# Attention and expert scaling on one core: scaling image by image, set-up in another order, two of TensorE's waits one product earlier

## The chip, the cores and the metric

The kernel runs on one core of a Trainium2 chip. The metric is the device time of one execution in microseconds, the median of several runs. Three runs of the kernel before took 686.49, 684.30 and 683.94 us, so its time is 684.3 us.

## What is computed

The input is a batch of 8 images of 128 channels with 48 x 48 tokens. Two layers follow one another, each with a residual:

```python
# x: (8, 128, 48, 48); 8 heads of 16; feature(t) = elu(t) + 1
y = ln_over_channels(x)
Q, K, V = feature(y Wq + bq), feature(y Wk + bk), y Wv + bv      # the 8 heads of a token
den = 1 / (sum_d Q * cumsum(K, axis=1) + 1e-10)                  # here the sum runs over the heads
num = causal linear attention of Q, K, V over the 2304 tokens    # S += k v^T; o = q S
x = x + num * den
t = tokens of x
z = ln(t)
p = softmax(z @ gate_w + router_gamma)                           # 8 experts, the best two are kept
combine = the two largest of p, the rest 0
out = t + sum_e combine_e * (gamma_e * (z @ expert_w_e + expert_b_e) + beta_e)
```

The running sum of the keys in `den` runs over the 8 heads, not over the tokens: the reference sums along that axis, and the kernel adds 8 blocks of 16 columns.

## The kernel before

The work is cut into **groups**: one group is four images (U = 4) by 128 tokens, and 18 chunks of tokens by two halves of the batch make 36 groups. Each engine runs a hand-written list, called a step. Step k of an engine handles pieces of several groups at once: `at(age)` gives group k - age, so a piece written under `at(5)` belongs to the group that is five steps old. The order inside a step is the order of the lines in `step`, and it is the same in every step. Ten steps are written out ahead of a loop, 26 run in the loop, two in each turn, and six stand behind it. Waits between engines are semaphore waits that `need` writes, always on a count of groups. In the written-out steps (`g.edge`) some more waits are written, which the loop doesn't need.

A group goes through these pieces. On TensorE `x_transposed`, then four projections `project` (L1005 to L1007, three products each, with high and low parts of the numbers), `key_values` (L1081), `q_transposed` and `k_transposed`, `scores` (L1062), `from_state` (L1099), `values` (L1116), `x1_centred` (L1138, input of the router), eight `experts` rows (L1212 to L1214: four images by two halves of the experts, "a" for experts 1 to 4 and "b" for 5 to 8), `coef_transposed` (L1152) and `output` (L1226 to L1231). `key_values`, `from_state` and `values` work on small tiles of the array and begin with a load of unused weights (`blank`), behind their waits.

VectorE takes the token statistics (`statistics` L649, `variances` L657), reads the projections (`project` L667), makes the features (L674), the denominators (L680 to L691), masks the scores (`causal` L696), adds attention and residual (`attention` L715), runs the router's chain of small operations (L726 to L809), adds the four experts 1 to 4 of each image with their scales (`experts_1_to_4` L824, 16 instructions in a group) and writes the result (`residual` L834).

ScalarE scales experts 5 to 8 (`scaled_by_scalar` L497, 16 instructions in a group), copies between memories, and takes exponentials and squares. GpSimd subtracts for the low parts (`x_low` L298, L365), makes deviations (L305 and L307, L352 and L354), the running sum of keys (L314, L317, L323), the normalised queries (`qn` L329), the state (`middle` L339, `state` L345), the low part of the packed coefficients (`pack` L359), and adds the scaled experts of two images in one instruction (`add_parts` L373). SP issues all loads and stores.

The names of the trace: `wide_a` and `wide_b` are the four PSUM banks that projections, scores and experts share, so that the next projection of a bank waits until VectorE has taken the experts out of it. `bank_g` and `bank_o` hold the transposes, the router's input and the output. In the set-up VectorE makes masks, clears five buffers (L590 to L594) and prepares the projection's weights (`w_t` L599, `w_high`, `w_low`), and all of the first group's work stands behind that. The second set of weights is prepared in the first steps: `expert_weights` (L639, L642) on VectorE behind the first `attention`.

## Time and profile before

| | |
|---|---|
| median of three runs | 684.3 us |
| the profiled execution | 687.47 us, its span 685.7 us |
| TensorE busy | 623.9 us (91% of the span) |
| VectorE busy | 626.5 us (91%) |
| ScalarE busy | 437.5 us (64%) |
| GpSimd busy | 501.6 us (73%) |
| SP's transfers | 15.5% of the 16 DMA engines' span |

The time of an execution is a little above its span, which runs from the first instruction to the last. Busy time is a share over all stages: the kernel has a fill of some 65 us until the first group is scaled, a long even stretch, and a drain in which fewer and fewer pieces of work are left. In the even stretch the granted clock of TensorE is 1.00. A row of an order of time gives start, length, engine and line. A length is that of the instruction and not of its share of the engine: instructions overlap in the engine's pipeline, so what one costs is read from the distance to the next start.

### The profile page before, as it was taken

The page shows a single profiled execution, that of the slowest core. Times are in us where ns is not written, and L with a number is a line of the kernel's source. Part 1 is how long each engine was busy: PE and PEld are TensorE (multiplying, and loading weights), DVE is VectorE, ACT ScalarE, POOL GpSimd, SP SyncE. Part 2 cuts the span into 40 slices and gives each one's busy share as a digit, 9 for nine tenths or more (in the row PEclk, how much of TensorE's full clock was granted, in tenths as well). Part 3 has the DMA queues.
Part 4 walks back from the last instruction along what each step waited for, and adds up shares of the span by engine and source line. Part 5 has one row for each costly group of instructions (what it writes and reads, how often), then busy time and mean ns, then how long its engine had stood idle before and what let it go on. Part 6 is the DMA issues. An engine that isn't in the chain of part 4 may idle for free.

```text
span 685.7 us, 37586 instructions
## 1 busy us (share of the span) xinstructions
PE 623.9 (91%) x13936; PEld 506.3 (74%) x14044; DVE 626.5 (91%) x2175; ACT 437.5 (64%) x1549; POOL 501.6 (73%) x745
## 2 busy tenths in 40 slices
PE   4769989999999999999999999999999999998875
PEld 3657777777777777777777777777777777777663
DVE  6778989999999999999999999999999999999774
ACT  1337656666667777666666667776776666667643
POOL 4747767777778888887778877878787787766631
PEclk9989999999999999999999999999999999999997
DMA  5211110111111111111111111111111121111001
GB/s 131 78 34 34 34 48 8 47 49 50 47 46 46 46 46 46 46 46 46 46 46 46 46 46 46 46 46 46 46 46 46 46 62 31 32 34 34 19 19 31
DMA packets 60234, 30.58 MB, mean 45 GB/s; under 512 B 2160, under 2 KB 60176, under 8 KB 60176
## 3 DMA queue, kind: packets, MB, share of 16 engines
q1 hardware_dynamic: 60176, 29.79, 15.5%
q8 instruction: 39, 0.64, 0.4%
q14 instruction: 19, 0.16, 0.1%
HBM read 20.34 MB, written 9.44 MB: 43 GB/s over the span
## 4 chain that ended last, share of the span: by engine, by line
PE 52%; DVE 24%; issue 15%; POOL 5%; DVEq 1%; ACT 1%; POOLq 0%; ACTq 0%
DVE total L824 4%; PE wide_b L1005 4%; PE num L1116 4%; PE wide_a L1212 4%; PE num L1081 3%; PE num L1099 3%; PE wide_a L1213 3%; PE wide_a L1214 3%; DVE bn L649 3%; DVE probs L696 3%; PE wide_a L1062 3%; DVE o L834 2%; PE bank_g L1037 2%; PE bank_g L975 2%; PE bank_g L1022 2%
## 5 line engine op out<-in xcount | busy, mean ns | idle before, releaser
L497 ACT ACTIVATE part<-wide_a,scale 128x128 f32<-128x128 f32 x576 | 156.3, 382 | 2.5 <-PE wide_a L1214 1.0
L373 POOL TENSOR_TENSOR two_sums<-part 128x512 f32<-128x512 f32 x72 | 92.9, 1290 | 32.0 <-ACT part L497 30.4
L1212 PE MATMUL wide_a<-e_high,x_high 128*128 128x512 f32 x216 | 97.8, 453 | 3.1 <-issue 1.1
L460 ACT ACTIVATE q_eo<-bank_g,parity 128x512 f32<-128x512 f32 x72 | 49.7, 690 | 67.5 <-PE bank_g L1037 67.5
L1214 PE MATMUL wide_a<-e_high,x_low 128*128 128x512 f32 x216 | 85.6, 396 | 0.0
L1213 PE MATMUL wide_a<-e_low,x_high 128*128 128x512 f32 x216 | 85.4, 395 | 0.0
L317 POOL TENSOR_TENSOR k_sum<-k_sum,feat 128x64 f32<-128x64 f32 x216 | 72.6, 336 | 16.9
L359 POOL TENSOR_TENSOR pack<-weight,pack 128x64 fp32r<-128x64 f32 x36 | 22.2, 616 | 77.1 <-ACT pack L505 77.1
L824 DVE SCALAR_TENSOR_TENSOR total<-wide_b,scale,total 128x128 f32<-128x128 f32 x216 | 58.8, 342 | 0.0
L824 DVE SCALAR_TENSOR_TENSOR total<-wide_a,scale,total 128x128 f32<-128x128 f32 x216 | 58.8, 342 | 0.0
L1212 PEld LDWEIGHTS wide_a<-e_high,x_high 128*128 128x128 f32 x216 | 41.6, 193 | 21.1 <-issue 17.2
L1116 PE MATMUL num<-probs,v_pad 64*32 64x64 f32 x4608 | 54.1, 225 | 2.4 <-issue 1.2
L674 DVE SCALAR_TENSOR_TENSOR feat<-ex,qkv 128x512 f32<-128x512 f32 x72 | 51.7, 718 | 0.0
L298 POOL TENSOR_TENSOR x_low<-x,x_high 128x512 fp32r<-128x512 f32 x36 | 47.0, 1305 | 4.6 <-ACT x_high L421 4.6
L448 ACT ACTIVATE k_t<-bank_g 128x512 f32<-128x512 f32 x36 | 21.5, 597 | 44.7 <-PE bank_g L1022 44.7
L427 ACT ACTIVATE ex<-qkv 128x512 f32<-128x512 f32 x72 | 44.6, 622 | 8.4 <-DVE qkv L667 8.3
L1116 PEld LDWEIGHTS num<-probs,v_pad 64*32 64x32 f32 x4608 | 47.8, 105 | 1.8 <-issue 1.4
L1062 PE MATMUL wide_a<-q_eo,k_t 32*64 32x128 f32 x1152 | 41.9, 275 | 7.0 <-issue 3.7
L323 POOL TENSOR_TENSOR qk<-k_sum,feat 128x512 f32<-128x512 f32 x36 | 45.9, 1276 | 2.8
L1214 PEld LDWEIGHTS wide_a<-e_high,x_low 128*128 128x128 f32 x216 | 40.9, 189 | 9.6
L667 DVE SCALAR_TENSOR_TENSOR qkv<-wide_a,rstd,b_qkv 128x384 f32<-128x384 f32 x72 | 43.7, 609 | 4.5 <-issue 3.6
L365 POOL TENSOR_TENSOR x_low<-x,x_high 128x512 fp32r<-128x512 f32 x36 | 46.1, 1280 | 0.0
(175 smaller groups left out, 2003.6 us busy)
## 6 DMA issues: line engine op xcount, KB each, us to landing
x<-in_x SPq DMA_DIRECT2D x36, 256.0 KB, 3.0
x_res<-in_x SPq DMA_DIRECT2D x36, 256.0 KB, 3.6
out<-o SPq DMA_DIRECT2D x36, 256.0 KB, 3.1
e_raw<-in_L_ffn_expert_w SPq DMA_DIRECT2D x1, 512.0 KB
beta_raw<-in_L_ffn_beta_w SPq DMA_DIRECT2D x1, 512.0 KB
w_raw<-in_L_conv_Wkv SPq DMA_DIRECT2D x2, 64.0 KB, 2.4
b_qkv<-in_L_conv_bkv SPq DMA_DIRECT2D x1, 128.0 KB, 5.9
w_raw<-in_L_conv_Wq SPq DMA_DIRECT2D x1, 64.0 KB, 2.6
```

Of the source, the lines that this page charges most:

```text
L298: tt(x_low[:, g.par], x[:, g.par], x_high[:, g.par].bitcast(F32), ALU.subtract)\
L317: tt(k_sum[:, :, h], k_sum[:, :, h - 1], f[:, :, 1, h], ALU.add).then_inc(S["cumsum"], 1)
L373: tt(two_sums[:, g.par, two], part[:, two, 0:2], part[:, two, 2:4], ALU.add).then_inc(S[f"two_sums{p}"], 1)
L460: nc.scalar.activation(q_eo[:, g.par, :, e], bank_g[:].rearrange("p (u t) -> p u t", t=T), copy, scale=parity[:, e:e + 1]).then_inc(S[done ...
L497: last = nc.scalar.activation(part[:, u, e], w_bank[B_BANK[u]][:, 128 * e:128 * e + 128], copy, scale=scale[:, g.par, u, 4 + e:5 + e])
L674: stt(feat[:, g.par, 2 * h:2 * h + 2], ex[:, 2 * h:2 * h + 2], 1.0, qkv[:, g.par, 2 * h:2 * h + 2, 0:256], ALU.min, ALU.max).then_inc(S[f" ...
L824: last = stt(total[:, g.par, u], w_bank[A_BANK[u]][:, 128 * e:128 * e + 128], scale[:, g.par, u, e:e + 1], before, ALU.mult, ALU.add)
L1062: last = mm(w_bank[h][at, T * u:T * u + T], k_t[rows, g.par, u, at], q_eo[rows, g.par, u, :, at], start=True, stop=True, skip_group_check= ...
L1116: last = mm(num[PAIR * h:PAIR * h + PAIR, first:first + SUB], v_pad[at, g.par, u, 2 * h + e], probs[at, g.par, h, u, e], start=False, stop ...
L1212: mm(out, x1_high[:, g.par, u], e_high[:, four], start=True, stop=False)
L1213: mm(out, x1_high[:, g.par, u], e_low[:, four], start=False, stop=False)
L1214: mm(out, x1_low[:, g.par, u], e_high[:, four], start=False, stop=True).then_inc(S[f"{'ab'[half]}_{u}"], 1)
```

## The change

The edits are these.

- **Unit steps for the scaling.** `experts_1_to_4` takes one image instead of a pair. Experts 1 and 2 are added onto the first half of the sum of ScalarE's parts and experts 3 and 4 onto the second half, in two partial totals, and `output` transposes the two totals of an image instead of a total and a half. `add_parts` on GpSimd adds the parts of one image, 256 elements, instead of a pair. Semaphores `two_sums`, `a_steps` and `a_sum` exist for each image.
- **Set-up.** GpSimd clears the state, the padded values and the coefficients, which VectorE did before, and VectorE copies the transposed weights ahead of the small placement copies.
- **One instruction to another engine.** The addition of 1e-10 to the denominators is done by ScalarE instead of VectorE.
- **TensorE's waits.** For `key_values` and `values` the waits stand in front of the last product of the row ahead (a projection, an expert's row), and their load of unused weights is left out. In the written-out steps both stay. `from_state` follows `scores` at once and keeps both.
- **Order.** All five engines get another order of the pieces in a step, and ages that fit it. On VectorE the ages of most pieces fall by one, which only says where its step begins. SP stores a result in the step of its group's age 6 instead of 9 and loads the residual at age 2 instead of 4.

The diff, cut; the lists of the steps are told by the rows of order below it.

```diff
@@ -291,17 +291,21 @@
             made(nc.gpsimd.memset(blank[:], 0.0))
             for e in range(EXPERTS):
                 made(nc.gpsimd.memset(order[:, :, e:e + 1], float(EXPERTS - e)))
+            made(nc.gpsimd.memset(state[:], 0.0))
+            for b in range(PAR):
+                made(nc.gpsimd.memset(v_pad[:, b], 0.0))
+                made(nc.gpsimd.memset(coef_t[:, b].bitcast(F32), 0.0))
...
-            def add_parts(g, p):
-                need(pool, f"part{2 * p}", g.i + 1)
-                need(pool, f"part{2 * p + 1}", g.i + 1)
+            def add_parts(g, u):
+                need(pool, f"part{u}", g.i + 1)
                 need(pool, "out_done", g.i - 1)
-                two = slice(2 * p, 2 * p + 2)
-                tt(two_sums[:, g.par, two], part[:, two, 0:2], part[:, two, 2:4], ALU.add).then_inc(S[f"two_sums{p}"], 1)
+                tt(two_sums[:, g.par, u], part[:, u, 0:2], part[:, u, 2:4], ALU.add).then_inc(S[f"two_sums{u}"], 1)
...
+            def denominators_eps(g):
+                need(act, "rden_done", g.i)
+                need(act, "den_sum", g.i + 1)
+                nc.scalar.activation(den1[:], den[:], copy, bias=1e-10).then_inc(S["den_eps"], 1)
...
@@ -586,20 +596,15 @@
                 for g in range(PAIRS):
                     rows = slice(PAIR * g, PAIR * g + PAIR)
                     copy(mask32[rows], heads_mask[rows, rows]).then_inc(done, 1)
-                for b in range(PAR):
-                    nc.vector.memset(v_pad[:, b], 0.0).then_inc(done, 1)
-                nc.vector.memset(state[:], 0.0).then_inc(done, 1)
                 nc.vector.memset(ins_window[:], 0.0).then_inc(done, 1)
-                for b in range(PAR):
-                    nc.vector.memset(coef_t[:, b].bitcast(F32), 0.0).then_inc(done, 1)
+                dve.wait_ge(S["first_pe"], 1)
+                copy(w_t[:], w_bank[0][:, 0:384]).then_inc(done, 1)
                 for n in range(2):
                     copy(place[:, n].rearrange("e (k j) -> e k j", j=2 * EXPERTS)[:, :, EXPERTS * n:EXPERTS * n + EXPERTS],
                          ident[0:EXPERTS, 0:EXPERTS].unsqueeze(1).broadcast_to([EXPERTS, EXPERTS, EXPERTS])).then_inc(done, 1)
-                dve.wait_ge(S["first_pe"], 1)
-                copy(w_t[:], w_bank[0][:, 0:384]).then_inc(done, 1)
                 dve.wait_ge(S["first_pe"], 2)
                 copy(w_high[:], w_bank[1][:, 0:384]).then_inc(done, 1)
-                dve.wait_ge(done, 19)
+                dve.wait_ge(done, W_READY - 1)
                 tt(w_low[:], w_bank[1][:, 0:384], w_high[:].bitcast(F32), ALU.subtract).then_inc(done, 1)
...
-            def experts_1_to_4(g, p):
+            def experts_1_to_4(g, u):
                 need(dve, "out_done", g.i - 1)
-                need(dve, f"two_sums{p}", g.i + 1)
+                need(dve, f"two_sums{u}", g.i + 1)
                 need(dve, "scale_done", g.i + 1)
-                need(dve, f"a_{2 * p}", g.i + 1)
-                need(dve, f"a_{2 * p + 1}", g.i + 1)
-                done = S[f"a_steps{p}"]
-                for e in range(4):
-                    for k in range(2):
-                        u = 2 * p + k
-                        if e > 0:
-                            dve.wait_ge(done, 6 * g.i + 2 * e - 1 + k)
-                        before = total[:, g.par, u] if e > 0 else two_sums[:, g.par, u, 0]
-                        last = stt(total[:, g.par, u], w_bank[A_BANK[u]][:, 128 * e:128 * e + 128],
-                                   scale[:, g.par, u, e:e + 1], before, ALU.mult, ALU.add)
-                        if e < 3:
-                            last.then_inc(done, 1)
-                last.then_inc(S[f"a_sum{p}"], 1)
+                need(dve, f"a_{u}", g.i + 1)
+                done, y = S[f"a_steps{u}"], w_bank[A_BANK[u]]
+
+                def add(e, before):
+                    return stt(total[:, g.par, u, e // 2], y[:, 128 * e:128 * e + 128], scale[:, g.par, u, e:e + 1], before,
+                               ALU.mult, ALU.add)
+
+                add(0, two_sums[:, g.par, u, 0]).then_inc(done, 1)
+                add(2, two_sums[:, g.par, u, 1]).then_inc(done, 1)
+                dve.wait_ge(done, 2 * g.i + 1)
+                add(1, total[:, g.par, u, 0])
+                dve.wait_ge(done, 2 * g.i + 2)
+                add(3, total[:, g.par, u, 1]).then_inc(S[f"a_sum{u}"], 1)
...
                 need(pe, "feat0", g.i + 1)
                 need(pe, "feat1", g.i + 1)
                 if first(g):
@@ -1071,7 +1081,11 @@
                 need(pe, "x1_done", g.i)
                 if g.edge:
                     need(pe, "kv_masked", g.i)
-                nc.tensor.ldweights(blank[:], tile_position=(0, 0))
+
+            def key_values(g, waited):
+                if not waited:
+                    key_values_ready(g)
+                    nc.tensor.ldweights(blank[:], tile_position=(0, 0))
...
                 mm(bank_o[:], eb_rows[:], coef_t[:, g.par], start=True, stop=False, skip_group_check=True)
                 for u in range(U):
-                    out = bank_o[:, T * u:T * u + T]
-                    mm(out, two_sums[:, g.par, u, 1], ident[:], start=False, stop=False, is_transpose=True,
-                       skip_group_check=True)
-                    last = mm(out, total[:, g.par, u], ident[:], start=False, stop=(u == U - 1), is_transpose=True,
-                              skip_group_check=True)
+                    if u == U - 1 and ahead:
+                        ahead()
+                    for k in range(2):
+                        last = mm(bank_o[:, T * u:T * u + T], total[:, g.par, u, k], ident[:], start=False,
+                                  stop=(u == U - 1 and k == 1), is_transpose=True, skip_group_check=True)
...
@@ step on TensorE, two places @@
+                g = at(2)
+                n = at(4)
+                early = bool(n and not n.edge)
+                if g:
+                    project(g, 2, (lambda: key_values_ready(n)) if early else None)
+                g = at(4)
+                if g:
+                    key_values(g, early)
...
+                g = at(5)
+                n = at(4)
+                early = bool(n and not n.edge)
+                if g:
+                    experts(g, 1, 1, (lambda: values_ready(n)) if early else None)
+                g = at(4)
+                if g:
+                    values(g, early)
```

On **VectorE**, in the loop, from the residual of a group to its next scaling; `o` is the residual, `x` the sum of attention and residual, `mv` the variances, `den` and `rden` the denominators, ISA and REGISTER_ALU rows are waits. Before:

```order
L834 TENSOR_TENSOR o<-bank_o,x 128x512
L712 REGISTER_ALU
L715 TENSOR_TENSOR x<-num,x_res 128x512
L183 REGISTER_ALU
L655 MEMSET pause 128x1
L657 BN_AGGR mv<-bn 128x2 x4
L674 SCALAR_TENSOR_TENSOR feat<-ex,qkv 128x512
L686 TENSOR_SCALAR den<-den 128x32
L691 RECIPROCAL rden<-den 128x32
L824 SCALAR_TENSOR_TENSOR total<-wide_b,scale,two_sums 128x128 x2
```

After, from the features on (the lines have other numbers):

```order
L679 SCALAR_TENSOR_TENSOR feat<-ex,qkv 128x512 x2
L183 REGISTER_ALU x2
L654 BN_STATS bn<-bank_g 128x6 x4
L832 REGISTER_ALU
L833 TENSOR_TENSOR o<-bank_o,x 128x512
L183 REGISTER_ALU
L660 MEMSET pause 128x1
L662 BN_AGGR mv<-bn 128x2 x4
L712 REGISTER_ALU
L715 TENSOR_TENSOR x<-num,x_res 128x512
L183 REGISTER_ALU
L685 TENSOR_REDUCE den<-qk 128x32
```

The variances now stand between residual and attention sum, both features stand ahead of the statistics, the denominators have lost the TENSOR_SCALAR, and behind this reduction of `den` come eight scalings, the reciprocal, eight more scalings, three projections, the masked key-value sums and the router's first product.

On **TensorE**, in the loop, around the key-value products (`num<-qkv,feat`); `wide_b<-w_high,x_high` and the two rows behind it are one projection. Before:

```order
L1005 MATMUL wide_b<-w_high,x_high 128x384
L1006 MATMUL wide_b<-w_low,x_high 128x384
L1007 MATMUL wide_b<-w_high,x_low 128x384
L183 ISA
L1074 LDWEIGHTS blank
L1081 MATMUL num<-qkv,feat 32x32 x32
```

After:

```order
L1007 MATMUL wide_b<-w_high,x_high 128x384
L1008 MATMUL wide_b<-w_low,x_high 128x384
L183 ISA
L1011 MATMUL wide_b<-w_high,x_low 128x384
L1095 MATMUL num<-qkv,feat 32x32 x32
```

The wait (ISA) has moved in front of the projection's third product, and the load of `blank` is gone.

On **GpSimd**, in the loop, from the low part of the packed coefficients to the subtraction for x1 (`x_low` of L365 before, L369 after); `ve` and `rstd` are a deviation, L305 and L307 (after: L309 and L311) of the first layer, L352 and L354 (after: L356 and L358) of the second. Before, from the normalised queries on:

```order
L329 TENSOR_TENSOR qn<-feat,rden 128x512
L183 REGISTER_ALU
L365 TENSOR_TENSOR x_low<-x,x_high 128x512
L352 TENSOR_TENSOR ve<-ss,eps 128x4
L354 TENSOR_TENSOR rstd<-ve,minus_half 128x4
L183 REGISTER_ALU
L339 TENSOR_TENSOR middle<-state,kv_new 128x128
L183 REGISTER_ALU
```

After:

```order
L309 TENSOR_TENSOR ve<-mv,eps 128x4
L311 TENSOR_TENSOR rstd<-ve,minus_half 128x4
L375 TENSOR_TENSOR two_sums<-part 128x256 x2
L333 TENSOR_TENSOR qn<-feat,rden 128x512
L356 TENSOR_TENSOR ve<-ss,eps 128x4
L358 TENSOR_TENSOR rstd<-ve,minus_half 128x4
L369 TENSOR_TENSOR x_low<-x,x_high 128x512
L183 REGISTER_ALU
L343 TENSOR_TENSOR middle<-state,kv_new 128x128
L183 REGISTER_ALU
```

Before, the subtraction for x1 stood ahead of the second layer's deviation; now it stands behind it, directly ahead of `middle`, and the parts are added in pieces of 256.

## Rows read from the trace of the kernel before

**Rows 1.** Residuals of the even stretch (instructions of L834), and the engines' busy time there

```profile
L834 DVE TENSOR_TENSOR o<-bank_o,x x24: 675/680/683, 190.3 to 591.9; 128x512 f32<-128x512 f32 x24
...
core 0: us, PE busy (x) PEld busy (x) DVE busy (x) ACT busy (x) POOL busy (x), PEclk, DMA share, GB/s
190.27:608.47 418.20, 400.44 (x9238) 327.12 (x9311) 403.44 (x1413) 288.04 (x1030) 332.42 (x480) 1.00 0.16 45
```

**Rows 2.** VectorE in order of time, one group: start, length, [idle before <-releaser]

```profile
398.36 0.89 DVE L649 BATCH_NORM_STATS2 bn<-bank_g 128x6 f32<-128x128 f32 x4
399.17 0.67 DVE L680 TENSOR_REDUCE den<-qk 128x32 f32<-128x512 f32 x1
399.75 0.68 DVE L834 TENSOR_TENSOR o<-bank_o,x 128x512 f32<-128x512 f32 x1
400.65 0.69 DVE L715 TENSOR_TENSOR x<-num,x_res 128x512 f32<-128x512 f32 x1 [0.22 <-DVE o L834]
401.27 0.18 DVE L657 BATCH_NORM_AGGREGATE mv<-bn 128x2 f32<-128x6 f32 x1
...
401.56 0.66 DVE L674 SCALAR_TENSOR_TENSOR feat<-ex,qkv 128x512 f32<-128x512 f32 x1
402.14 0.18 DVE L686 TENSOR_SCALAR den<-den 128x32 f32<-128x32 f32 x1
402.35 0.35 DVE L691 RECIPROCAL rden<-den 128x32 f32<-128x32 f32 x1
```

**Rows 3.** TensorE (PE) and its weight loads (PEld) in order of time, same stretch

```profile
397.91 0.09 PEld L1109 LDWEIGHTS <-blank 128*32 128x32 bf16 x1 [0.36 <-issue]
...
403.85 0.40 PE L1214 MATMUL wide_a<-e_high,x_low 128*128 128x512 f32 x1
404.78 0.44 PE L1005 MATMUL wide_b<-w_high,x_high 128*128 128x384 f32 x1 [0.54 <-DVE total L824]
```

**Rows 4.** TensorE's transposed coefficients and ScalarE's rows of the same group

```profile
399.43 0.33 PE L1152 MATMUL bank_g<-ident,pack 128*128 128x128 f32 x1
...
392.84 0.23 ACT L484 ACTIVATE pexp<-lgm 128x32 f32<-128x32 f32 x1 [0.94 <-DVE lgm L742]
...
397.87 2.17 ACT L497 ACTIVATE part<-wide_a,scale 128x128 f32<-128x128 f32 x8
399.88 1.09 ACT L515 ACTIVATE coef_t<-bank_g 32x128 fp32r<-32x128 f32 x4
```

**Rows 5.** One feature instruction of VectorE, and GpSimd at the same time

```profile
627.29 1.68 DVE L674 SCALAR_TENSOR_TENSOR feat<-ex,qkv 128x512 f32<-128x512 f32 x1
...
627.12 1.30 POOL L373 TENSOR_TENSOR two_sums<-part 128x512 f32<-128x512 f32 x1 [1.49 <-ACT part L497]
```

**Rows 6.** GpSimd's instructions in order of time, even stretch and (last row) drain

```profile
388.20 1.29 POOL L365 TENSOR_TENSOR x_low<-x,x_high 128x512 fp32r<-128x512 f32 x1
...
390.72 0.46 POOL L339 TENSOR_TENSOR middle<-state,kv_new 128x128 f32<-128x128 f32 x1
...
397.97 0.65 POOL L359 TENSOR_TENSOR pack<-weight,pack 128x64 fp32r<-128x64 f32 x1 [2.04 <-ACT pack L505]
...
641.67 0.32 POOL L359 TENSOR_TENSOR pack<-weight,pack 128x64 fp32r<-128x64 f32 x1 [1.77 <-ACT pack L505]
```

**Rows 7.** The fill in order of time: TensorE, VectorE, GpSimd

```profile
4.91 0.85 PE L930 MATMUL wide_a<-ident,w_raw 128*128 128x128 f32 x3
...
8.67 0.54 DVE L599 COPY w_t<-wide_a 128x384 f32<-128x384 f32 x1
...
47.62 0.51 POOL L305 TENSOR_TENSOR ve<-mv,eps 128x4 f32<-128x4 f32 x1 [6.75 <-issue]
...
52.48 0.62 DVE L667 SCALAR_TENSOR_TENSOR qkv<-wide_a,rstd,b_qkv 128x384 f32<-128x384 f32 x1 [2.54 <-issue]
```

**Rows 8.** The chain of waits in the drain: start, length on the chain, engine and line

```profile
632.56 1.23 POOL x_low L365
...
649.25 1.22 POOL x_low L365
...
663.35 1.29 POOL two_sums L373
664.73 2.17 DVE total L824 x8
```

382 lines of the change are left out of this document (195 added, 187 removed).

## The prediction

> **What bounds the kernel now.** I read the busy time of the engines in the long even stretch first, then VectorE's own order of work in one group, then what TensorE, ScalarE and GpSimd wait for around it. In the stretch from 190.27 to 608.47 us there are 24 groups, seen by their 24 residual additions, so one group takes 418.20 / 24 = 17.43 us; VectorE is busy for 403.44 us of it, 16.81 us a group, TensorE for 400.44 us and GpSimd for 332.42 us, 13.85 us a group [rows 1]. VectorE and TensorE are nearly equal by that, so the order in a group decides between them. TensorE starts its last product of the scoring of experts at 403.85 us and the next projection only at 404.78 us, after an idle 0.54 us that ends with VectorE's scaled sum [rows 3]. VectorE shows one such gap in a group, 0.22 us ahead of the sum of attention and residual, and what it waits for there is its own previous instruction [rows 2]. So **VectorE sets the pace**, and an edit on another engine is worth nothing until VectorE has to wait for it.
>
> **What leaves VectorE.** (1) The small addition of 1e-10 to the denominators goes to ScalarE. It took the time from 402.14 to 402.35 us, 0.21 us a group [rows 2]. (2) Before, the residual is followed at once by the attention sum, which must see the residual's own output written: 400.65 - 399.75 = 0.90 us pass between the two starts, and then the variances take 401.56 - 401.27 = 0.29 us [rows 2]. Now the variances stand between the two. The 0.90 us remain, the variances lie inside them, and 0.29 us go. (3) The sixteen scalings by experts 1 to 4 keep their number and size. Two partial sums run side by side in each image, so each instruction still waits for the one two places ahead, as before. I count nothing. (4) In the chain of the router's small operations I count 11 neighbours of which the second needs the first, before and after; nothing again. Together 0.50 us a group.
>
> **What may come back.** (5) Both feature instructions now stand back to back right behind the scales, and ScalarE's and GpSimd's work on the packed coefficients starts at the same moment. A feature instruction that began at 627.29 us lasted 1.68 us, not the 0.66 us of the one at 401.56: a GpSimd addition ran from 627.12 to 628.42 us, and the feature went on from there [rows 2, 5]. In the other direction GpSimd's pack took 0.65 us beside a feature, and 0.32 us in the drain where none ran [rows 6]. So the second feature loses between 0 us (it starts first) and 0.33 us (GpSimd does). I take 0.15 us. The Trainium skill, SBUF — State Buffer, section "Who interferes with whom", says that a VectorE instruction with two SBUF inputs and a GpSimd instruction that reads SBUF exclude each other, and that the first to start holds the port to its end; the trace agrees, with 1.68 against 0.66 us. (6) The reciprocal of the denominators now needs ScalarE, where its addition stands behind all four scaled images. Both ways start at bn_stats. On VectorE it is 0.81 (399.17 - 398.36) + 0.90 + 0.62 (401.27 - 400.65) + 0.58 (399.75 - 399.17) + eight scalings of 2.17 together = 5.08 us until the reciprocal's turn [rows 2, 8]. The other way is bn_stats 0.89, the transposed coefficients on TensorE 0.33, their copies on ScalarE 1.09, eight scaled parts 2.17 and the addition, priced by a ScalarE instruction of the same shape, 0.23: 4.71 us [rows 2, 4]. Four handovers come on top, one of which is 399.88 - 399.76 = 0.12 us [rows 4], so about 5.1 us. The two are level, the wait is between 0 and 0.2 us, and I take 0.05 us, nearer to nothing, since GpSimd's pack and ScalarE are early there.
>
> So a group gains 0.50 - 0.15 - 0.05 = **0.30 us**. Of the 36 groups 24 lie in the stretch, six ahead of it and six behind. I give the price to the first 30: 9.0 us, between 0 (the waits eat it all) and 15.0 us (no wait at all). The last six belong to the drain.
>
> **What I cost at nothing.** GpSimd adds the scaled parts in four instructions of 256 elements for two of 512. No row has that size: 128 elements took 0.46 us, 512 took 1.30 us [rows 5, 6], and the line between them gives an estimate of 0.74 us. GpSimd gets 4 x 0.74 - 2 x 1.30 = 0.36 us more (from -0.76 to 2.60 us by the two rows), 14.2 us a group, under VectorE's. TensorE loses two loads of unused weights; the one ahead of the values had 0.36 us of waiting before it [rows 3]. But TensorE stands idle for VectorE anyway, so this only widens its room. Behind the moved waits stands the last product of a projection or of an expert's row, and behind that VectorE's reading of it. What is waited for (features, masked scores, padded values, the sum of the group ahead) is done by then in my order of the group, so the cost is nothing; if not, VectorE is late by the same time. On SP the store and the residual load move to an earlier step and block the next load of x until the sum of attention is done. The load still comes almost a whole group ahead of its use.
>
> **The start.** VectorE's five clearing instructions go to GpSimd. VectorE copies the transposed weights at 8.67 us, though TensorE had them from 4.91 + 0.85 = 5.76 us on [rows 7]. At most 2.9 us go; I take 2.5 us, since the biases and the second load must land too. Later in the fill GpSimd stands 6.75 us ahead of the fourth group's deviation (the row names no releaser; by the order it needs variances that stand behind the preparation of all expert weights). The normalised queries stand behind it on GpSimd, and VectorE then stands 2.54 us ahead of the projection behind these [rows 7]. Now the variances come before that preparation. I take 1.5 us of the 2.54. The fill gains 4.0 us, between 1.0 and 5.4 us.
>
> **The drain.** In its last rounds GpSimd's subtraction for x1 stands ahead of the deviation that the router waits for, and the chain of waits runs through it twice, 1.23 us at 632.56 and 1.22 us at 649.25 us [rows 8]. Now the deviation comes first: 2.4 us. At the very end one image's sum (0.74 for the pair's 1.29 us) and four scalings instead of eight (half of 2.17 us) lie on the chain: 0.55 + 1.09 = 1.6 us [rows 8]. Together 4.0 us, between 2 us (another wait is close behind) and 7 us (the last two rounds gain as much again).
>
> **The sum.** 9.0 + 4.0 + 4.0 = 17.0 us. The profiled execution took 687.47 us by its own time, 685.7 us of span, and would take 670.5 us. It stood 3.2 us above the median of 684.3 us, so I forecast 684.3 - 17.0 = **667 us**. Its own range is 658 to 676 us: from 15.0 + 4.0 + 7 = 26 us to 5.0 (a third of the steady part's most) + 1.0 + 2 = 8 us.
>
> **Rivals.** *No wait at all.* VectorE keeps all of 0.50 us and fill and drain give their most: 15.0 + 5.4 + 7 = 27.4 us, 657 us. For it speaks that VectorE hardly waits now and that GpSimd has room; against it the level race in (6). *The gain turns into a wait.* A loop through TensorE (scores start only when the last projection is read, and the projections only behind all the scaled sums) or through (6) holds the old 17.43 us, and only fill and drain remain: 684.3 - 8.0 = 676 us, or 681 us where these give only their lower ends. For it speaks TensorE's small idle time of 0.54 us in a group; against it that this idle time ends with VectorE. *VectorE is caught behind a long GpSimd instruction, and the kernel is slower.* The router's first product, with both inputs in SBUF, now stands right behind the masked key-value sums, and on GpSimd the subtraction for x1 (1.29 us [rows 6]) stands right ahead of the instruction that waits for these sums. If GpSimd runs late, the subtraction is under way just when the product wants to start. One such catch cost 1.68 - 0.66 = 1.02 us [rows 2, 5]. Once a group this makes -0.30 + 1.02 = 0.72 us, 30 x 0.72 = 21.6 us, less 8.0 us: 13.6 us slower, 698 us. It decides from 0.30 us a group for the steady part and from 0.30 + 8.0 / 30 = 0.57 us for the whole. GpSimd's additions near 1.30 us would bring it about; against it stand GpSimd's 14.2 of about 17.1 us. By the Trainium skill's same section the holder is whoever starts first, so this rival and (5) are one rule at two places; taken with its full 0.33 us, (5) alone gives 30 x 0.18 = 5.4 us less, 672.7 us.
>
> **How the numbers follow.** My forecast 0.48, no wait at all 0.13, the wait in its place 0.22, the catch 0.17. About 0.5% (3.4 us) is what a measurement of this kernel can tell from no change. Faster by more: 0.48 + 0.13 + two thirds of the wait (0.15) = 0.76. Within: 0.07 of the wait and 0.01 of a mild catch, 0.08. Slower: 0.16. The range of 8 in 10 leaves out half of the best case and most of the catch: 655 to 685 us.
>
> **What would show it.** In the changed profile a group of the even stretch should take 17.1 us (16.9 without a wait), with VectorE busy almost throughout and the variances inside the time between residual and attention sum. (5) shows as a feature instruction near 1.0 us, (6) as idle time ahead of the reciprocal that ScalarE ends, the catch as a product of over 1 us. GpSimd's new additions should take 0.74 us. The copy of the transposed weights should start at about 6 us, and the last rounds should have no subtraction for x1 in the chain of waits. I am wrong if a group takes 17.4 us or more, or if VectorE waits for TensorE's projections.

## The result, and the profile after

The changed kernel takes **754.0 us** (747.8 to 757.4, four runs) against 684.7 us: a ratio of 1.0998, interval 1.0912 to 1.1083, so 10% slower. I had forecast 667 us with a range of 655 to 685. The mechanism is none of my rivals. Of the runs below one, of b_pad382 (746.5 us), fell in the slower state that some executions of a kernel show, and it is left out.

The page of the changed kernel, first its shares and the slices (tenths), then its DMA queues (packets, MB, share):

```profile
span 755.2 us, 37724 instructions
PE 640.2 (85%) x13936; PEld 521.1 (69%) x13992; DVE 632.8 (84%) x2134; ACT 449.1 (59%) x1585; POOL 517.5 (69%) x822
PE   4669999998978896989888897989798968989885
PEclk9887999999989999999989998999999989999998
q8 instruction: 93, 1.52, 0.9%
```

The same queue in the kernel before:

```profile
q8 instruction: 39, 0.64, 0.4%
```

Every engine is busy about as long as before and the span is 69.5 us longer; all of them wait. The queue that brings instructions has 54 packets more, and 1.52 MB / 93 is 16 KB each. In the trace all 54 lie inside the loop, nine in each of six of its 13 turns, while before has none there. (A turn of the loop is two groups.)

Five turns in a row of the changed kernel, cut at TensorE's loop turn: stretch and its length, then busy us (x instructions) of PE, PEld, DVE, ACT, POOL, TensorE's granted clock, the DMA engines' busy share and GB/s:

```profile
260.50:296.40 35.90, 34.49 (x772) 28.33 (x774) 32.09 (x107) 23.95 (x85) 26.45 (x43) 0.95 0.15 42
296.40:340.60 44.20, 34.97 (x776) 28.60 (x774) 35.76 (x126) 25.82 (x92) 29.80 (x46) 0.96 0.14 39
340.60:375.30 34.70, 33.08 (x791) 27.18 (x775) 32.04 (x107) 23.77 (x85) 27.31 (x44) 1.00 0.16 45
375.30:420.00 44.70, 36.02 (x762) 29.42 (x751) 35.00 (x122) 25.07 (x90) 29.57 (x45) 0.92 0.14 38
420.00:456.00 36.00, 33.26 (x795) 27.41 (x797) 32.80 (x112) 24.56 (x89) 27.59 (x45) 1.00 0.16 44
```

Long and short turns alternate. The chain of waits through one long turn (start, length on the chain, what) shows the extra time:

```profile
295.04 1.41 PE num L1138 x91
296.45 5.10 issue
301.55 0.79 PE wide_b L1238
302.34 0.43 PE wide_b L1239
...
318.51 1.36 PE num L1138 x88
319.88 1.49 issue
321.37 0.31 PE num L1138 x5
...
334.19 0.93 issue
335.12 0.31 PE num L1117 x6
...
339.27 1.07 issue
340.34 0.42 PE num L1138 x23
```

L1138 are the products of the values, the last piece of TensorE's list; L1238 the first product of the next turn. Between them TensorE stands 5.10 us, in "issue": nothing that the profile shows ends it. But two of the turn's nine instruction packets start in this stretch (296.4 to 301.5 us):

```profile
q8 instruction: 2, 0.03, 4.2%
```

Three smaller holes follow, **in the middle** of rows of small products (5, 6 and 23 products are left over), where no wait stands at all. The four make 8.6 us. For the whole of 200 to 660 us TensorE's longest waits are (engine line <- what ended it: us, times, longest):

```profile
PE wide_b L1238 <- issue: 31.4, 11, 5.2
PE num L1138 <- issue: 16.5, 11, 1.8
PE num L1117 <- issue: 7.4, 15, 1.2
```

Before, from 190 to 610 us, TensorE waited for VectorE, and hardly for anything else:

```profile
PE wide_b L1005 <- DVE total L824: 12.1, 23, 0.5
```

Behind the 5.10 us in which TensorE stood idle, its granted clock is 0.52 and 0.51 from 301.5 to 305 us, the lower of its two levels (1.2 GHz), and 1.00 again (2.4 GHz) from 305 us on: the product at 302.14 us took 0.63 us for 0.39 in a_pad130 below, at full clock.

### The profile page after: what moved, and what is told of

Same layout as the page of the kernel before. It is cut to its first block, busy times and chain, and to the rows that moved or that the text cites. A ratio compares the mean times of both kernels' runs of the same rounds, so it can differ in the third digit from the quotient of the medians.

```text
span 755.2 us, 37724 instructions
## 1 busy us (share of the span) xinstructions
PE 640.2 (85%) x13936; PEld 521.1 (69%) x13992; DVE 632.8 (84%) x2134; ACT 449.1 (59%) x1585; POOL 517.5 (69%) x822
## 3 DMA queue, kind: packets, MB, share of 16 engines
q8 instruction: 93, 1.52, 0.9%
## 4 chain that ended last, share of the span: by engine, by line
PE 67%; DVE 17%; issue 14%; POOL 1%; DVEq 1%; ACT 1%; ACTq 0%; POOLq 0%
PE wide_a L1238 7%; PE wide_a L1242 6%; PE wide_a L1239 6%; PE num L1138 6%; DVE probs L696 4%; PE wide_b L1238 3%; PE bank_g L1162 3%; PE num L1095 3%; PE num L1117 3%; PE wide_b L1007 3%; PE wide_b L1242 2%; PE wide_b L1239 2%; PE bank_g L1045 2%; PE bank_g L977 2%; PE wide_a L1072 2%
## 5 line engine op out<-in xcount | busy, mean ns | idle before, releaser
L375 POOL TENSOR_TENSOR two_sums<-part 128x256 f32<-128x256 f32 x144 | 104.3, 734 | 95.0 <-ACT part L508 94.3
L1238 PE MATMUL wide_a<-e_high,x_high 128*128 128x512 f32 x216 | 103.0, 477 | 8.8 <-DVE probs L696 6.1
L1242 PE MATMUL wide_a<-e_high,x_low 128*128 128x512 f32 x216 | 88.6, 410 | 0.9 <-issue 0.9
L1239 PE MATMUL wide_a<-e_low,x_high 128*128 128x512 f32 x216 | 88.7, 411 | 0.0
L321 POOL TENSOR_TENSOR k_sum<-k_sum,feat 128x64 f32<-128x64 f32 x216 | 70.7, 328 | 16.9
L819 DVE SCALAR_TENSOR_TENSOR total<-wide_b,scale,two_sums 128x128 f32<-128x128 f32 x144 | 43.5, 344 | 46.1 <-PE wide_b L1242 41.2
L524 ACT ACTIVATE coef_t<-bank_g 32x128 fp32r<-32x128 f32 x144 | 38.8, 269 | 72.1 <-PE bank_g L1178 70.8
L466 ACT ACTIVATE q_eo<-bank_g,parity 128x512 f32<-128x512 f32 x72 | 45.6, 685 | 51.0 <-PE bank_g L1045 51.0
L1138 PE MATMUL num<-probs,v_pad 64*32 64x64 f32 x4608 | 56.9, 225 | 20.4 <-issue 20.1
L1138 PEld LDWEIGHTS num<-probs,v_pad 64*32 64x32 f32 x4608 | 48.6, 105 | 32.0 <-issue 31.9
L1238 PE MATMUL wide_b<-e_high,x_high 128*128 128x512 f32 x72 | 36.3, 504 | 31.8 <-issue 31.7
L1238 PEld LDWEIGHTS wide_a<-e_high,x_high 128*128 128x128 f32 x216 | 43.3, 201 | 28.2 <-issue 17.4
L327 POOL TENSOR_TENSOR qk<-k_sum,feat 128x512 f32<-128x512 f32 x36 | 60.1, 1670 | 0.0
L369 POOL TENSOR_TENSOR x_low<-x,x_high 128x512 fp32r<-128x512 f32 x36 | 46.4, 1288 | 0.0
```

The source lines that it names most:

```text
L321: tt(k_sum[:, :, h], k_sum[:, :, h - 1], f[:, :, 1, h], ALU.add).then_inc(S["cumsum"], 1)
L327: tt(qk[:], k_sum[:].rearrange("p u h d -> p u (h d)"), feat[:, g.par, :, 0:128], ALU.mult)\
L369: tt(x1_low[:, g.par], x1[:, g.par], x1_high[:, g.par].bitcast(F32), ALU.subtract)\
L375: tt(two_sums[:, g.par, u], part[:, u, 0:2], part[:, u, 2:4], ALU.add).then_inc(S[f"two_sums{u}"], 1)
L1138: last = mm(num[PAIR * h:PAIR * h + PAIR, first:first + SUB], v_pad[at, g.par, u, 2 * h + e], probs[at, g.par, h, u, e], start=False, stop ...
L1238: mm(out, x1_high[:, g.par, u], e_high[:, four], start=True, stop=False)
```

## First question: is it the loop's place in TensorE's code?

TensorE's program is straight code for ten steps, a loop of two steps, and straight code for six. The change deals its list out afresh, so fewer instructions lie ahead of the loop: the loop's first and its closing instruction are number 5104 and 6721 of the program before, and 5042 and 6656 after. 39 packets for a program of 10,104 instructions, and 32 for 8,425 in a_peel8 below, make one packet for 259 to 263 instructions; I took 256, and 6656 is 26 times 256. So the first theory was: a closing branch on the **edge** of a piece of code is bad. Four kernels:

```diff
+                for _ in range(130):
+                    pe.wait_ge(S["first_pe"], 1)
                 pe.wait_ge(S["first_dve"], W_T)
```

a_pad130 is the changed kernel with these fulfilled waits (two make one instruction); b_pad382 the kernel before with 382 of them, a_pad2 the changed kernel with 2.

> The changed kernel with 130 waits that are already fulfilled, written ahead of TensorE's first use of w_t in the start. They become 65 instructions of TensorE (two waits share one), nothing else changes, and the loop's closing branch moves from place 6656 of TensorE's program to 6721, where it stands in the kernel before. Theory of the place (TensorE's code is brought by the instruction queue in pieces of 16,384 bytes, 256 instructions; where the branch falls on the edge of a piece, the loop's code is not kept and is brought again every second turn): the branch takes 0.2 us in every turn, the instruction queue q8 carries 39 or 40 packets, not 93, no row of L1238 on wide_b waits 5 us for issue, and the time falls to my old forecast of 667 us, between 655 and 685. Rival of the order (the loop now turns right behind the many small products of the values, which the sequencer can't feed in time, wherever it lies): 93 packets, 4.7 to 5.2 us ahead of every second turn, 745 to 757 us.

> The kernel before with 382 fulfilled waits (191 TensorE instructions) at the same point of the start: its branch moves from place 6721 to 6912, which is 27 times 256, as 6656 is 26 times 256 in the changed kernel. Nothing of the change is in it. The waits themselves cost the start up to 7 us (191 at some 0.05 us less the 3.7 us that TensorE stands idle there). Theory of the place: about 93 packets on q8, the branch takes about 5 us in every second turn, and the time is 684 + 56 to 70 us, that is 740 to 755 us. Rival of the order: the old order keeps its pace, 684 to 692 us, 39 or 40 packets.

> The changed kernel with two fulfilled waits (one TensorE instruction) in the start: branch at place 6657, the second instruction of a piece. Narrow form of the place: 39 packets, 655 to 685 us. Wide form, or the rivals of order and of the waits: 93 packets, 745 to 757 us.

a_loads restores the waits and loads that the change moved:

```diff
-                early = bool(n and not n.edge)
+                early = False
```

> The changed kernel with the waits of the key-value and value rows back at their own heads and the unused load behind them in the loop too, as in the kernel before; order and everything else as changed. The body grows by four instructions, the loop begins at the same place, and the branch stands at 6660 instead of 6656. Rival of the waits (moving the waits to the last product of the row ahead, without the load between, is what starves TensorE): 39 packets and 665 to 690 us. Theory of the place in its narrow form (only a branch on the very first instruction of a piece is bad): the same, 665 to 690 us. In its wide form (a branch shortly behind the edge is bad as well): 93 packets, 745 to 757 us. a_pad2 and a_pad130 then tell the first two apart.

Measured: a_pad130 693.9 us (39 packets), b_pad382 732.3 (76), a_pad2 750.7 (93), a_loads 752.6 (93). Sixty-five idle instructions ahead of the loop take 60 us away, though not down to the 655 to 685 that I had expected. 191 of them ahead of the old loop add 46.8 us to the 685.5 of the kernel before; 17.9 of these are their own (TensorE's product with `w_t` starts at 27.12 us for 9.27: 191 at 0.11 us, not the 0.05 that I assumed, less 3.5 of idle time), and 29 remain. That is fewer than in the changed kernel and under my 740 to 755 us, since here only four of the 13 turns bring their code again (36 packets). The order of the work and the moved waits are cleared. a_pad130's turns:

```profile
352.30:386.90 34.60, 33.01 (x774) 27.18 (x774) 33.50 (x117) 24.73 (x89) 28.54 (x45) 1.00 0.17 45
386.90:421.50 34.60, 33.01 (x775) 27.15 (x774) 33.49 (x117) 24.76 (x89) 28.53 (x45) 1.00 0.16 45
```

All turns are alike, with the clock at 1.00. Two turns of the changed kernel (375.3 to 456.0) take 80.7 us for these 69.2: 11.5 us, and six such pairs make 69. Next the limits of the bad stretch, by 32 and 96 waits, and, in a_peel8 (below) with 290, ahead of an edge:

> The changed kernel with 32 fulfilled waits, 16 TensorE instructions: branch at 6672, 16 behind the edge. It brackets where the place turns good, between 4 (93 packets in a_loads) and 65 (39 packets in a_pad130). If what counts is that the next piece has been asked for and has come before the branch is reached (a packet takes 0.9 to 1.4 us, and 65 of the small products of the values last about 1.5 us), 16 are too few: 93 packets and 748 to 755 us. If a handful is enough: 39 packets and 690 to 695 us.

> The changed kernel with 96 fulfilled waits, 48 TensorE instructions: branch at 6704, 48 behind the edge, between 16 (93 packets) and 65 (39 packets). If a packet must have been asked for and have landed by the time the branch is reached, this is near the limit; I lean to good: 39 packets and 691 to 695 us. If the limit lies above 48: 93 packets, 750 to 767 us.

> a_peel8 with 290 fulfilled waits, 145 TensorE instructions: branch at 5107, 13 ahead of the next edge at 5120. It tells whether only the stretch behind an edge is bad or both sides of it. If the branch must not fall while a piece is on its way, this one, 243 behind the last edge, is good: about 33 packets, and 685.4 us and up to 12 more for the waits (145 at 0.11 us less 3.7 us of idle time): 690 to 700 us. If the nearness of an edge is bad on either side, because the loads run ahead of the instruction in hand: 80 packets or more, 740 us and over.

Measured: 767.0 us (93 packets; the 13 us over the changed kernel stay unexplained), 693.6 (39) and 758.4 (87). The last is against me: 13 **ahead** of an edge is bad too. A second theory fits all places so far: what counts is the **span**, how many pieces the loop touches; seven are kept and eight are not. It needs the edges 30 to 61 instructions earlier than I counted (an estimate from a_pad96 being good and a_pad32 bad; some start-up code may stand ahead of the program, which no row shows). The holes in the rows of small products say the same without this fit: counted through the program, in every long turn of the changed kernel they lie just ahead of instructions 5842, 6353 and 6610, and all three are edges if these stand 47 earlier than multiples of 256 (5888, 6400, 6656). Two kernels set edge and span against each other. a_short leaves out, in the loop, the values' products of two of four images; b_long adds waits to the loop of before:

```diff
-                    for e in range(2):
+                    for e in range(0 if u < 2 and not g.edge else 2):
...
+                for _ in range(0 if g.edge else 240):
+                    pe.wait_ge(S["first_pe"], 1)
                 mm(bank_o[:], eb_rows[:], coef_t[:, g.par], start=True, stop=False, skip_group_check=True)
```

> The changed kernel with the products of the values left out for two of the four images of a group, in the loop alone: 256 TensorE instructions fewer in a turn (these images lack the attention inside a block there). The loop begins at the same place, 5042, and its branch falls on 6400, 25 times 256, again on an edge. Theory of the edge (what counts is where the branch stands against the edge, -13 to 16 bad, 48 and more good): the code comes again every second turn, about 80 packets, branches of 4 to 5 us. Theory of the span (what counts is how many pieces the loop touches: seven are kept, eight are not; with some 30 to 61 instructions that the runtime puts ahead of the program all ten places tried so far come out by it): 5042 to 6400 touches seven, so no piece comes again, about 38 packets, every branch 0.2 us, and 670 to 690 us.

> The kernel before with 240 fulfilled waits, 120 TensorE instructions, ahead of the output of each group in the loop, so 240 instructions more in a turn. The waits cost some 13 us a group (120 at 0.11), so the time says nothing by itself; the packets and the branches do. The branch falls on 6961, 49 behind an edge. Theory of the edge: good, as in a_pad96 (48 behind), 39 or 40 packets, branches of 0.2 us. Theory of the span: 1858 instructions can't lie in seven pieces of 256 (1792) wherever they begin, so the code comes again in the loop, 85 packets or more, and the branch takes 3 us or more in every second or third turn.

a_short, on an edge but seven pieces long: 680.0 us and

```profile
q8 instruction: 38, 0.62, 0.4%
```

b_long, off the edge but eight pieces long:

```profile
q8 instruction: 148, 2.42, 0.9%
```

Both come out by the span. Pieces are counted here with edges 45 earlier (47 gives the same); the times are medians of two to ten runs, of b_long one run:

| kernel | loop, first to last | pieces | packets | median us |
|---|---|---|---|---|
| before | 5104 to 6721 | 7 | 39 | 684.7 |
| after | 5042 to 6656 | 8 | 93 | 754.0 |
| a_pad2 | 5043 to 6657 | 8 | 93 | 750.7 |
| a_loads | 5042 to 6660 | 8 | 93 | 752.6 |
| a_pad32 | 5058 to 6672 | 8 | 93 | 767.0 |
| a_pad96 | 5090 to 6704 | 7 | 39 | 693.6 |
| a_pad130 | 5107 to 6721 | 7 | 39 | 693.9 |
| a_peel8 | 3348 to 4962 | 7 | 32 | 685.4 |
| p_pad290 | 3493 to 5107 | 8 | 87 | 758.4 |
| b_peel8 | 3414 to 5031 | 7 | 32 | 683.6 |
| b_pad382 | 5295 to 6912 | 8 | 76 | 732.3 |
| a_short | 5042 to 6400 | 7 | 38 | 680.0 |
| b_long | 5104 to 6961 | 8 | 148 | 1101.4 |

The Trainium skill, Runtime: NRT & Kernel Launch, section "Instruction fetch mechanics", gives TensorE room for 2048 instructions, refilled in blocks of 256, and says that a taken branch whose target isn't in the current window of two pages waits for a fetch. The traces agree on the wait, with 0.3 us ahead of the first product of a turn in a kept loop and up to 4.9 to 5.2 us in the changed kernel and its forms that aren't kept, but not on the window: loops that touch seven blocks turn without a fetch, and those that touch eight don't. Why seven and not eight, no run shows. The page also says that the cost of going on straight from block to block is mostly hidden; here rows of small products stop for up to 1.8 us at the edges while code comes in.

## Second question: what is the rest of the change worth?

a_peel8 writes out eight steps ahead of the loop for ten, which moves the loop without any added instruction; b_peel8 is the same with the kernel before.

```diff
-            first = (depth + 4) // PAR
+            first = (depth + 2) // PAR
```

> The changed kernel with eight written-out steps ahead of the loop for ten, on every engine, so the loop makes 14 turns for 13; no wait added, no order changed. TensorE's closing branch falls on place 4962 of its program, 98 instructions behind the edge of a piece (19 times 256 is 4864). Theory of the place: no piece is brought again in the loop, about 33 packets on q8, every branch 0.2 us. Since the 65 instructions of a_pad130 lay on the path of the start (TensorE's product with w_t began at 13.07 us there and at 9.43 us in the changed kernel), the time is that of a_pad130 less 3.6 us: 690 us, give or take 2. If the place were only part of it and the padding had helped in another way (by delaying the start of TensorE against the others), the time is near 750 us.

> The kernel before with eight written-out steps ahead of the loop for ten, nothing else: what the peeling itself is worth, to set beside a_peel8. TensorE's branch falls on 5031, 167 behind an edge. a_peel8 took 685.4 us where I expected 690 from a_pad130, so the shorter straight code may be worth some 4 us of its own; then this kernel takes 681 us. If the difference was only in the changed kernel's start, 685 us. By the theory of the place no piece comes again in the loop, about 32 packets.

685.4 us, ratio 1.0008 (0.9989 to 1.0026), and 683.6, ratio 0.9988 (0.9975 to 1.0002). So **with the place mended the change is worth nothing**: 1.7 us more than before with the same peeling. (By a_pad130, with ten steps, it is even 5.6 us slower: 690.3 us, which is 693.9 less the 3.6 by which the waits delay the start. I expected 690 and 681; why ten steps cost the changed kernel 5 us and the old one 1 wasn't settled.) The even stretch of 24 groups, a_peel8 then b_peel8:

```profile
191.20:607.40 416.20, 395.79 (x9259) 325.89 (x9286) 403.20 (x1390) 296.17 (x1052) 340.94 (x528) 1.00 0.16 45
```

```profile
184.80:601.80 417.00, 399.58 (x9243) 327.65 (x9317) 402.16 (x1413) 288.16 (x1030) 332.98 (x480) 1.00 0.16 45
```

With spans of 682.6 and 681.6 us the change makes the fill 6.4 us longer, the 24 groups 0.8 us shorter in all, and the drain 4.6 us shorter (75.2 for 79.8). With ten steps, a_pad130 against before, the three are 3.5 longer (without the waits' 3.6), 3.6 shorter and 2.3 longer, so only the longer fill and a shorter stretch hold in both pairs.

**The fill.** VectorE's first copies and GpSimd's clearings in the changed kernel:

```profile
3.08 3.56 DVE L589 TENSOR_SCALAR centre<-ident 128x128 f32<-128x128 f32 x1 [3.08 <-POOL minus_half L287]
3.36 4.60 DVE L595 COPY tri<-tri 64x64 f32<-64x64 f32 x2
3.79 0.95 POOL L296 MEMSET v_pad<- 128x1024 f32 x1
...
8.83 0.54 DVE L601 COPY w_t<-wide_a 128x384 f32<-128x384 f32 x1
```

Before, the first two took 0.61 and 0.63 us and the weights were copied at 8.67 us [rows 7]. The clearings left VectorE's queue and came back as VectorE's wait behind GpSimd's long writes (3.79 to 6.57 us). a_late moves the preparation of the expert weights behind the reciprocal (it had stood ahead of the denominators); a_start is a_late with `v_pad` and `coef_t` cleared not on GpSimd but on VectorE, in its idle time at 20 us (both diffs, cut):

```diff
             def gammas_and_gate():
+                for b in range(PAR):
+                    nc.vector.memset(v_pad[:, b], 0.0).then_inc(S["clears"], 1)
+                    nc.vector.memset(coef_t[:, b].bitcast(F32), 0.0).then_inc(S["clears"], 1)
                 dve.wait_ge(S["rest_pe"], 1)
...
                     inverse_denominators(g)
                     if first(g):
                         router()
+                g = at(4)
+                if g and first(g):
+                    expert_weights()
```

> a_peel8 with VectorE's preparation of all expert weights (3.8 us, once) behind the first reciprocal of the next group, where the change puts it ahead of the denominators. Theory of the start: in the changed kernel the denominators of the second group stand at 53.78 us behind this preparation, before at 42.14 us ahead of it, and the chain of waits runs denominators, reciprocal, normalised queries, TensorE. So the fill gets 3 to 6 us back: 684 to 687 us. Rival: TensorE's first scoring of experts waits for the weights then, and nothing is gained: 690 us.

> a_late with the clearing of v_pad and coef_t off GpSimd and on VectorE again, but at 20 us, where VectorE stands idle for some 3 us ahead of the copies for gammas and gate. Theory of the port: GpSimd's clearings at 3.5 to 6.6 us are what made VectorE's first copies last 3.4 to 4.6 us for 0.5 to 0.6; without them the transposed weights are copied at about 6 us and not at 8.83 us, and the whole is 2.5 us shorter than a_late. Rival: the load of the second block of x or of the biases ends last there, and nothing is gained.

a_late 685.0 us against a_peel8's 685.4: nothing, as the rival had it. a_start 681.9: 3.1 us for the 2.5 expected, and in its trace

```profile
3.36 0.87 DVE L593 COPY tri<-tri 64x64 f32<-64x64 f32 x2
...
6.11 0.54 DVE L599 COPY w_t<-wide_a 128x384 f32<-128x384 f32 x1
```

The clearings cost 0.16 us of the longer fill (the copy at 8.83 for 8.67 us) and the gain that I had counted on. Most of the rest stands at one place: TensorE's transposes of the fourth group's `x` begin at 30.68 us for 25.22 (30.31 for 24.98 in a_peel8 and b_peel8). The transposes of the first group's keys ahead of them are late already (26.57 us for 23.89), since they wait for VectorE's statistics, which now stand behind the copies for gammas and gate. A hole of 3.49 us in "issue" follows at 27.20 us. In the kernel the transposes of `x` wait for ScalarE's copy of the transposed keys, and this copy now stands behind the exponentials of the next group. Before, and then after:

```profile
24.52 0.60 ACT L448 ACTIVATE k_t<-bank_g 128x512 f32<-128x512 f32 x1 [2.89 <-PE bank_g L1022]
25.22 0.63 PE L975 MATMUL bank_g<-ident,x 128*128 128x128 f32 x4 [0.73 <-issue]
```

```profile
30.01 0.58 ACT L454 ACTIVATE k_t<-bank_g 128x512 f32<-128x512 f32 x1
30.68 1.08 PE L977 MATMUL bank_g<-ident,x 128*128 128x128 f32 x4 [3.49 <-issue]
```

No run moved these two pieces alone, so what their place is worth isn't shown.

**The even stretch.** b_var has one edit, the variances ahead of the attention sum in the kernel before. a_router gives a_start's router the old order; a_feat is a_router with the second feature behind the attention sum.

```diff
                     residual(g)
+                g = at(0)
+                if g:
+                    variances(g)
                 g = at(4)
                 if g:
                     attention(g)
                     if first(g):
                         expert_weights()
-                g = at(0)
-                if g:
-                    variances(g)
```

> The kernel before with one thing of the change alone: VectorE's variances between the residual and the sum of attention, two pieces exchanged on VectorE. TensorE's program is word for word that of before, so its loop keeps its place. My step 2: 0.29 us less in each group, 30 groups, 8.7 us: 676 to 677 us. Rival: VectorE or another engine waits in their place (TensorE's 0.54 us of idle time in a group shows how near it is), and the time stays within 2 us of 685.

> a_start with VectorE's small router operations in the order of the kernel before: the masked scores stand behind the first logits (L758) and behind the maximum of others again, and the sums of exponentials between the later ranks. Nothing else moves. In the steady groups these rows with the two masked scores take 5.93 us a group in the kernel before and 6.18 us in a_peel8, where my step 4 said no difference. If that is the order, a group goes from 17.33 to about 17.1 us and the time from 682 to 673 to 676 us. Rival: the difference is the loop turn of VectorE or ScalarE's exponentials, wherever the rows stand, or TensorE (16.5 us a group) ends last now: 680 to 682 us.

> a_router with the second feature instruction behind the sum of attention again, as in the kernel before, so that the two no longer stand back to back. My step 5: back to back they take 1.34 us for 1.19 us. If the neighbour is the cause, 0.15 us a group, 30 groups, 4.5 us less than a_router. Rival: the feature meets GpSimd at its new place too, or the work that waits for it (TensorE's transposes, GpSimd's sums of keys) is late by the same time: a_router's time, give or take 1 us.

b_var 682.2 us, ratio 0.9948 (0.9930 to 0.9966): 3.4 us for the 8.7 expected. a_router 680.6, 1.4 us less than a_start for the 6 to 9 expected, as its rival had it: the order of the small rows is not it. a_feat 685.7, 5.1 us more than a_router: the feature met GpSimd in its new place too, here in order of time,

```profile
382.69 1.90 POOL L372 TENSOR_TENSOR two_sums<-part 128x256 f32<-128x256 f32 x2 [0.33 <-ACT part L506]
383.13 0.86 DVE L680 SCALAR_TENSOR_TENSOR feat<-ex,qkv 128x512 f32<-128x512 f32 x1
```

0.86 us for 0.66, and GpSimd's two additions 1.90 for the 1.43 that they take in a_pad130. Last, b_best sets steps 1 and 2, the late clearing and the peeling into the kernel before (its diff is cut to step 1); b_two is b_best without step 1.

```diff
+            def denominators_eps(g):
+                need(act, "rden_done", g.i)
+                need(act, "den_sum", g.i + 1)
+                nc.scalar.activation(den1[:], den[:], copy, bias=1e-10).then_inc(S["den_eps"], 1)
...
                     coefs(g)
+                g = at(3)
+                if g:
+                    denominators_eps(g)
+                g = at(5)
+                if g:
                     scaled_by_scalar(g, 3)
```

> The kernel before, with its own order on TensorE, GpSimd and SP, and only those edits of the change that the runs so far leave standing: the variances between residual and attention (b_var: 682.2 us), the 1e-10 on ScalarE, there ahead of the last scaled image, the clearing of v_pad and coef_t on VectorE at 20 us (a_start), and eight written-out steps. If my steps 1 and 2 add up, a group gains 0.21 us more than in b_var: 682.2 - 1.2 (peeling) - 2.9 (start) - 30 x 0.21 = 672 us. Rival: the reciprocal now waits for ScalarE, or TensorE, whose idle time shrinks from 0.5 to 0.3 us a group in b_var, ends last, and steps 1 and 2 give together no more than 2 alone: 678 us.

> b_best without the 1e-10 on ScalarE: the kernel before with the variances between residual and attention, the clearing of v_pad and coef_t on VectorE at 20 us, and eight written-out steps. In b_best VectorE waited 0.7 us a group for GpSimd's sums, which wait for the scaled part that the 1e-10 delays on ScalarE. If that is what cost b_best its gain, this kernel takes 682.2 (b_var) - 1.2 (peeling) - 2.9 (start) = 678 us. If not, it is near b_best's 687 us.

b_best 687.6 us, ratio 1.0041 (1.0025 to 1.0058); b_two **678.5**, ratio 0.9904 (0.9884 to 0.9924), the fastest kernel here and faster than both given ones. VectorE's waits in b_best, and then in b_var:

```profile
DVE total L829 <- POOL two_sums L373: 16.9, 23, 0.8
```

```profile
DVE total L824 <- POOL two_sums L373: 2.1, 13, 0.2
```

The addition takes 0.23 us on ScalarE ahead of the last scaled image; GpSimd's sum waits for that image, and VectorE for the sum, 0.73 us a group. In the old order these are level already in b_var; in b_two, which lacks step 1 alone, the wait is 1.9 us in all for 16.9.

## Why the prediction was wrong, step by step

**The step that failed** stands under "What I cost at nothing": TensorE's part of the change got no cost, since "TensorE stands idle for VectorE anyway, so this only widens its room". It looked at TensorE's rows and waits, and had no term for where the loop lies in the code. The runs show 64 us for it (754.0 less 690.3, which is a_pad130's 693.9 without the 3.6 us by which its waits delay the start), of a loss of 69. That VectorE sets the pace held only as long as every other engine is fed. And with the loop kept, the sum's largest term failed too: the even stretch gained 0.8 us (a_peel8 against b_peel8), or 3.6 (a_pad130 against before), for 7.2, which is what its 24 groups have of my 9.0.

For the stretch, VectorE's rows of a_peel8, two groups in turn, against before [rows 2]:

```profile
399.67 0.67 DVE L833 TENSOR_TENSOR o<-bank_o,x 128x512 f32<-128x512 f32 x1
...
401.17 0.68 DVE L685 TENSOR_REDUCE den<-qk 128x32 f32<-128x512 f32 x1
...
410.29 0.32 DVE L758 SCALAR_TENSOR_TENSOR lg<-hot,lgm 128x32 f32<-128x32 f32 x1
410.64 0.19 DVE L762 TENSOR_REDUCE top<-lg 128x4 f32<-128x32 f32 x1
...
414.70 1.42 DVE L679 SCALAR_TENSOR_TENSOR feat<-ex,qkv 128x512 f32<-128x512 f32 x2
416.05 0.88 DVE L654 BATCH_NORM_STATS2 bn<-bank_g 128x6 f32<-128x128 f32 x4
416.85 0.67 DVE L833 TENSOR_TENSOR o<-bank_o,x 128x512 f32<-128x512 f32 x1
```

Start to next start, averaged over 20 groups of each kernel:

- (1) The addition off VectorE: -0.21 us as forecast. It holds in the changed order, where ScalarE does it behind all four images, and turns into a wait in the old one (b_best).
- (2) Residual to the end of the attention sum: -0.23 for -0.29. The 0.90 us of [rows 2] stand in every second group alone; in the others it was 0.72. b_var nets 0.18 (414.0 us for 24 groups, 418.2 before).
- (3) Scaling: -0.06 for 0. (6) Reciprocal: -0.06 for +0.05; no wait for ScalarE. (My four handovers make 4.71 + 0.48 = 5.19 us and not 5.1; it changes nothing here.)
- (4) Router with the masked scores: **+0.26 for 0**. Counting dependent neighbours is not enough: L762 starts 0.35 us behind L758, where most such neighbours are 0.22 apart, and before a masked score stood between them. But a_router, with the old order, gains only 0.03 a group over a_start (414.4 for 415.2 us in 24). Every second group takes 0.4 us more (416.85 - 399.67 = 17.18, the next 17.57; before 17.3 and 17.5 on average). VectorE's own loop turn now lies in this chain; that it is the cause was only argued.
- (5) Features: +0.16 for +0.15. With the projections' +0.06 the sum is about -0.09 for -0.30.
- GpSimd's additions of 256: 0.734 us for my 0.74.
- The start: 6.4 us longer for 4.0 shorter. For the clearings I had looked at which engine clears, not at what it locks meanwhile; for the rest I had not priced VectorE's and ScalarE's new order in the fill. The Trainium skill's rule on the shared port (SBUF — State Buffer, "Who interferes with whom"), which I used for the features, names copies too, in their two-port mode. That these copies run in that mode no row shows; the times fit the rule, with 4.60 us beside the clearings, 0.63 before and 0.87 in a_start.
- The drain: 4.6 us for 4.0, which is luck as far as the runs show. The subtraction for x1 is gone from the changed kernel's chain, but b_peel8's chain doesn't hold it either, and with ten steps the drain is 2.3 us longer (79.6 for 77.3).

With a kept loop the forecast would still have missed: 685 to 690 us, at the upper edge of the range or above it. Of my rivals the one in which the gain turns into a wait comes nearest, with 681, but by its number only: in a_peel8's stretch VectorE shows no wait, and its own rows took the gain back.

## What to carry to other kernels

Before moving instructions on an engine whose loop nearly fills its instruction store, count its instructions in the loop and ahead of it: the profile's instruction queue tells at once (39 packets or 93) whether the loop is kept, and idle time named "issue" at the loop's turn, or in the middle of a row of small products, is code on its way if packets of that queue start there. By itself "issue" says nothing: the 3.49 us in the fill end with ScalarE's copy. If a loop falls badly, change the number of written-out steps ahead of it before judging anything else. And compare an edit with the old kernel only at a place where both loops are kept; otherwise the place is what is measured.

## What the hardware showed that I had not expected

- A TensorE loop of 1615 instructions runs without any code transfer where it touches seven pieces of 256, and costs 11.5 us in two turns where it touches eight (changed kernel against a_pad130). Shortening it by 256 on the same start cures it (a_short).
- The penalty is not only the jump (5.1 us): while code comes in, rows of small products (95 in 1.16 us) stop for up to 1.8 us, and behind the 5.1 us the granted clock is 0.52, so that a long turn has 0.92 to 0.96 on average.
- Fulfilled waits are not free: 65 instructions of two waits each held TensorE for 7.05 us at the start of a_pad130, 0.11 us each, where it had stood idle for 3.67.
- GpSimd's row of clearings of 512 and 1024 elements a partition (2.8 us in all) holds up VectorE's first instructions, which last 3.56 and 4.60 us for 0.61 and 0.63.
